# One fused two-branch kernel on one core: TensorE's mask matmuls moved from between the two halves of P times V to behind them, directly ahead of projection chunks 2 and 3

## What is computed

```python
def attn_layer(x, Wqkv, qs, ksc, Wo):          # 16 heads of 64, windows of 32
    q, k, v = jnp.split(x @ Wqkv, 3, -1)
    q = l2norm(q) * qs ; k = l2norm(k) * ksc   # then rotary with xpos scale
    ...
    out = local_attention(q, k, v)
    return out @ Wo

def local_attention(q, k, v):                  # each window sees itself and the one before
    ...
    mask = (it < jb) | (it > jb + w) | (jb == -1)
    sim = jnp.einsum('bhwie,bhwje->bhwij', bq, bk2) * QK_SCALE
    sim = jnp.where(mask, -jnp.finfo(sim.dtype).max, sim)
    attn = jax.nn.softmax(sim, -1)
    out = jnp.einsum('bhwij,bhwje->bhwie', attn, bv2)

for i in range(6):
    x = attn_layer(shift_tokens(x), ...) + x
    x = ffn_layer(shift_tokens(x), ...) + x
```

## Time and profile before

| | us |
|---|---|
| median of 3 runs | 1634.78 |
| lowest and highest run | 1634.45, 1636.02 |
| the profiled execution, whole | 1636.79 |
| its span, first to last instruction | 1634.9 |
| busy in the span: PE, DVE, ACT, POOL | 1595.2, 1396.1, 1338.8, 1321.5 |

### The profile page before, as it was taken

The page is one execution under the profiler, slowest core; times in us unless marked ns, Lnnn a source line. Parts: engine busy times, 40 slices in busy tenths (PEclk is TensorE's granted clock), DMA queues, the critical chain, the costliest instruction groups (busy, mean ns, idle before and its releaser), DMA issues.

```text
span 1634.9 us, 50862 instructions
## 1 busy us (share of the span) xinstructions
PE 1595.2 (98%) x19920; PEld 1369.1 (84%) x19920; DVE 1396.1 (85%) x2021; ACT 1338.8 (82%) x2516; POOL 1321.5 (81%) x1278
## 2 busy tenths in 40 slices
PE   5899999999999999999999999999999999999997
PEld 3778888888888888888888888888888888888886
DVE  7788888888888888888888888888888899999975
ACT  5768888788888878888888888888888888888874
POOL 8888899888889888889888889888888777767741
PEclk9999999999999999999999999999999999999999
DMA  4334233433323344232344324244332332222232
GB/s 136 106 116 140 70 98 88 118 109 98 107 74 95 97 122 117 77 108 73 95 111 129 99 73 111 70 121 109 110 95 76 85 98 77 78 73 70 64 89 58
DMA packets 184872, 156.89 MB, mean 96 GB/s; under 512 B 111551, under 2 KB 156093, under 8 KB 184637
## 3 DMA queue, kind: packets, MB, share of 16 engines
q1 hardware_dynamic: 184636, 153.64, 33.7%
HBM read 27.56 MB, written 1.05 MB: 17 GB/s over the span
## 4 chain that ended last, share of the span: by engine, by line
PE 87%; ACT 5%; DVE 2%; issue 2%; POOL 2%; DMA 1%; SPq 0%; ACTq 0%; POOLq 0%; DVEq 0%
PE ps_pv L802 12%; PE ps_s L778 10%; PE ps_pv L821 10%; PE ps_tr L739 9%; PE ps_qn L714 9%; PE ps_qn L715 7%; PE ps_qn L716 7%; PE ps_tr L726 5%; PE ps_pv L811 3%; PE ps_qn L901 2%; PE ps_s L761 2%; PE ps_qn L902 2%; PE ps_qn L903 2%; PE ps_pv L859 1%; PE ps_qn L888 1%
## 5 line engine op out<-in xcount | busy, mean ns | idle before, releaser
L2027 POOL TENSOR_TENSOR qk<-qk,t 128x1024 f32<-128x1024 f32 x192 | 455.8, 2376 | 82.2 <-DVE qk L1545 81.6
L1542 DVE TENSOR_TENSOR t<-ps_qn,tab 128x512 f32<-128x512 f32 x384 | 264.4, 689 | 122.8 <-ACT sq L1140 111.5
L2039 POOL TENSOR_TENSOR qkr<-qk,rinv 128x1024 f32<-128x1024 f32 x192 | 361.5, 1904 | 8.0 <-POOL rinv L2019 0.8
L714 PE MATMUL ps_qn<-w_hi,xs_hi 128*128 128x512 f32 x576 | 261.1, 453 | 10.7 <-DVE qk L1545 8.2
L1127 ACT ACTIVATE pbd<-ps_tr 64x512 f32<-64x512 f32 x384 | 226.0, 589 | 55.2 <-PE ps_tr L726 51.4
L1545 DVE TENSOR_TENSOR qk<-ps_qn,tab 128x512 f32<-128x512 f32 x384 | 261.0, 680 | 0.0
L1140 ACT ACTIVATE sq<-ps_qn 128x512 f32<-128x512 f32 x384 | 228.6, 595 | 33.1 <-PE ps_qn L716 28.4
L1173 ACT ACTIVATE qbd<-ps_tr 64x512 f32<-64x512 f32 x384 | 226.9, 591 | 33.5 <-PE ps_tr L739 28.0
L715 PE MATMUL ps_qn<-w_lo,xs_hi 128*128 128x512 f32 x576 | 230.2, 400 | 0.0
L716 PE MATMUL ps_qn<-w_hi,xs_lo 128*128 128x512 f32 x576 | 229.7, 399 | 0.0
L1555 DVE TENSOR_REDUCE ss<-sq 128x32 f32<-128x2048 f32 x96 | 216.6, 2256 | 0.0
(11 more groups left out here) (177 smaller groups left out, 3180.6 us busy)
## 6 DMA issues: line engine op xcount, KB each, us to landing
v_own<-v_new SPq DMA_DIRECT2D x96, 512.0 KB, 3.3
v_back<-v_new SPq DMA_DIRECT2D x96, 384.0 KB, 3.5
v_back<-v_own SPq DMA_DIRECT2D x94, 128.0 KB, 2.3
kT<-kT SPq DMA_DIRECT2D x84, 128.0 KB, 2.8
w_raw<-in_Wqkv SPq DMA_DIRECT2D x18, 512.0 KB, 5.1
rot<-in_rot SPq DMA_DIRECT2D x48, 128.0 KB, 2.7
fx<-xmid SPq DMA_DIRECT2D x96, 64.0 KB, 2.1
xsh<-x SPq DMA_DIRECT2D x190, 32.0 KB, 2.6
```

The costliest lines, as they stand in the source:

```text
L714: mm(ps_qn[bank][:, :], xs_hi[b][:, :], w_hi[:, part], start=True, stop=False)
L1542: v.tensor_tensor(t2[:, part].rearrange("p (h s d) -> p h s d", s=2, d=DH // 2), swapped, tab[:, 2 * k + 1:2 * k + 2, :].rearrange("p o (s ...
L2027: g.tensor_tensor(qk[b][:, part], qk[b][:, part], t2[:, part], ALU.add).then_inc(added[b], 1)
L2039: g.tensor_tensor(qkr[b][:, part].rearrange("p (h d) -> p h d", d=DH), qk[b][:, part].rearrange("p (h d) -> p h d", d=DH), rinv[b][:, k * ...
```

## The change

In TensorE's `half`, `mask(i, b)` changes places with `probs_v(i, b, 1)`. Nothing is added or removed, no other engine's program differs, and the drain keeps its order.

```diff
@@ -979,8 +979,8 @@
                     if (i.n, b) == (1, 1):
                         transpose_pair(1)
                     probs_v(i, b, 0)
+                    probs_v(i, b, 1)
                     mask(i, b)
-                    probs_v(i, b, 1)
                     qkv(i, b, (2, 3))
                     if i.first and b == 0:
                         pe.wait_ge(s_xT, 1)
```

## The result

The changed kernel takes **1652.34 us** (median of four runs, 1652.26 to 1653.51); the kernel before took 1635.4 us beside it (1634.45 to 1636.45). The ratio is 1.010, with a 95% interval of 1.0088 to 1.0113: 16.9 us slower. The prediction said 1648.5 us with a range of 1642 to 1656, and slower with a chance of 0.85. The profiled execution took 1652.3 us, its span is 1650.5 us, 15.6 us more than before.

A forecast was written before the change was run, and what follows sets the result against it. TensorE, busy 98%, was taken to bound the kernel, waiting for ScalarE's copies at the second half of P times V. 91 halves by 0.15 us = 13.7 us on 1634.8 gave 1648.5 us, range 1642 to 1656.

The forecast's parts named there:

- The gate: ScalarE's second pair of copies into `pbd` holds the second half of P times V until 0.06 us after their end.
- step 1: Mask gone from between the P times V halves: second half starts 0.12 us earlier, the other 0.30 us become idle.
- Rival A: At the second half of P times V: copies do not gate, time stays at 1634.8 us; chance 7%.
- Steps 2 and 3: Second half's last group 0.87 us after its first, mask 0.22 us later, chunk 2 0.32 us later (bounds 0.235, 0.41).
- Step 4: Chunk 2's first matmul takes 0.32 us, then 0.47 to chunk 3, whose second matmul is 0.135 or 0.165 us late.
- The covered wait of chunk 3: Chunk 3 no longer waits for VectorE's taking of chunk 1; its first matmul takes 0.235 us instead of 0.29.
- Step 5: Behind chunk 3: the softmax chain has room, other engines move with TensorE, so what follows costs nothing further.
- rival D: Later chunk 2 delays ScalarE and VectorE, costing in full: 91 halves by 0.21 = 19.1 us, 1653.9 us; chance 16%.
- B, both gates off: VectorE's taking of chunk 1 moves forward too: 92 halves by 0.16 = 14.7 us faster, 1620.1 us; chance 4%.
- C, the mask slipping into the wait: TensorE runs the mask ahead of the held second half of P times V, so the time stays; chance 3%.

The follow-up runs named there:

- The runs with early release: Kernel before, one `pbd` copy left out, replacement copy to an unread tile behind ScalarE's release: old order 1642.61 us (ratio 1.0041), mask moved 1636.24 us (0.9998).
- with the copy shortened: Kernel before, second copy of the second `pbd` pair left out, nothing in its place: old order 1634.28 us (ratio 0.9984), mask moved 1624.44 us (0.9925).

## Why the prediction was right, and where it was off

**The gate (how the kernel is bound, and step 1): right.** The copies let TensorE start 0.05 us after their end, the second half started 0.12 us earlier, and 0.30 us of the old mask's time became idle. The runs with early release show the cause and not only the coincidence: with it the loss of 16.9 us goes to nothing. Rival A needed the copies not to gate; they end where they did, and the second half starts right behind them. One thing was left out: in b = 0 halves the first copy also follows directly on ScalarE's work on the norms (819.61 + 0.23 = 819.84, the copy at 819.85), so there two paths end together. It changed nothing, since the copies start 0.75 us behind the transposes in either kind of half, before and after.

**Steps 2 and 3: right.** From the start of the second half to the mask it is 1.08 us (0.87 + 0.22 = 1.09 predicted), from the mask to chunk 2 0.32 us as taken. The bounds of 0.235 and 0.41 us were not needed.

**Step 4: right in mechanism, slightly under.** The first matmul of chunk 2 takes 0.33 to 0.34 us and not 0.32. Behind this mask it is as slow as behind P times V; the 0.30 us of the earlier trace rows, behind a long wait, was the wrong neighbour. The covered wait of chunk 3 came as predicted. In b = 0 the half is 0.15 to 0.16 us longer where 0.135 was said.

**Step 5, nothing downstream: wrong in the b = 1 halves, and in b = 0 at the end.** In b = 1 0.20 us were lost where 0.165 was said. About 0.17 is TensorE's own; the rest comes over ScalarE's squares, the table load, the copies of keys, the activation of the feed-forward chunk and VectorE's release of chunk 4's bank. That is rival D with its mechanism right, in these halves in nearly its full size (0.20 us, where D said 0.21), and in the b = 0 halves of this part not at all. At the end of the run it is the other way round. There chunk 4 of a b = 0 half keeps 8.42 to 8.43 us from the square of chunk 2 before and after, and 8.57 with the replacement copy, so D's path sets it and the whole 0.20 is lost; in b = 1 it keeps 9.37 us from TensorE's own second matmul of chunk 3, and 0.16 is lost.

**The sum: close.** Predicted were 91 halves by 0.15 = 13.7 us. The trace has 88 by 0.177 = 15.6 us, and the first halves took theirs up. For 88 halves the prediction's 0.15 gives 13.2 us. Of the 2.4 us above that, some 1.3 lie in the b = 1 halves, 0.7 in b = 0, and 0.5 in b = 0 at the end, as an estimate from these lengths. The medians differ by 16.9 us, 1.3 more than the spans, because the profiled execution of the kernel before (1636.79 us) lay 1.4 us above its median of now (1635.4).

**Rivals.** B, both gates off, was given 4% for this kernel and did not happen. But its price for a half was right: 0.16 us was said, and with the copy shortened the order after gained 0.15 to 0.16 us in the b = 1 halves and in those at the end, and nothing in the other b = 0 halves. C, the mask slipping into the wait, shows nowhere: the mask stands behind the second half in all 92 halves.

No version that does the whole work beat the kernel before by more than can be told. One that frees both gates without leaving work out was not tried. Open are, beside that, the 0.13 us by which the exponential came late in the runs with the replacement copy, and the 0.05 us by which P times V started late without the mask.

## What to carry to other kernels

Work that stands between two dependent pieces is to be priced by the wait that it covers and not by its busy time: taking this mask out altogether won 0.1%, and moving it by one place cost 1%. Before moving such work, look at the distance from the releasing engine's end to the start that follows it; where that is hardly more than the shortest seen (0.18 us here, against 0.05), the work ahead is filling a wait. And when a small wait further on seems to pay a loss back, look in every kind of iteration for an engine that takes the later data elsewhere. Here the path over the other engines ended 0.05 to 0.08 us later than TensorE's own in one kind of half, and earlier in the other.

## What the hardware showed unexpectedly

- A change of cut costs twice. The gap from one group to the next is 0.10 us longer (0.22 instead of 0.117 ahead of the mask, 0.33 instead of 0.235 behind a projection), and the first matmuls behind it are 0.05 to 0.11 us slower (0.17 instead of 0.117 for the first group of P times V; 0.34 instead of 0.235 for 512 columns; 1.89 instead of 1.78 for the group of L821).
- The mask's two matmuls of 512 columns each, in the upper and the lower 64 rows, take 0.32 us together with the change of cut behind them, and a second such pair adds 0.22 us. That is about the 0.235 us of one free matmul of 512 columns in the projection, so the two of a pair run beside each other.
- The replacement copy on ScalarE, from `ident` to bf16, took 0.63 us where the copy from PSUM to fp32 took 0.59, and the exponential later in the same half came 0.13 us late, for no reason that the trace shows. Source and type changed together, so which of them costs what isn't shown.
